# A sequence mixer and a ternary feed-forward layer on one core: Omega between the feed-forward blocks, and token sums from a context that DMAs add up in place

## The chip, the cores and the metric

One NeuronCore of a Trainium2 chip. The metric is device time in microseconds of one execution.

## What is computed

A batch of 16 sequences of 1024 tokens, 256 channels, goes through two sublayers. Cut to what matters:

```python
# mixer, on xn = layernorm(x)
omega = einsum('bsd,ed->bse', xn, W_omega) + b_omega
phi = cumsum(omega * exp(log_scale) / sqrt(position), axis=1)
cm_real, cm_imag = xn * cos(phi), xn * sin(phi)
mem_real = cumsum(cm_real, axis=1) / position
mem_imag = cumsum(cm_imag, axis=1) / position
ret_real = mem_real * cos(phi) + mem_imag * sin(phi)
ret_imag = mem_imag * cos(phi) - mem_real * sin(phi)
context = concatenate([cm_real, cm_imag, ret_real, ret_imag])   # 1024 wide
h = layernorm(context, ln_gamma, ln_beta) @ W1.T + b1           # to 512
x1 = x + xn + gelu(h) @ W2.T + b2                               # to 256
# feed-forward part, weights quantised to -1, 0, 1
out = x1 + relu(layernorm(x1) @ Wq1.T + b1) @ Wq2.T + b2        # 256 to 1024 to 256
```

## The kernel before

The tokens are cut into 32 chunks of 512, two to a sequence; sums that run over a sequence carry their last column from the even chunk to the odd one. Every fp32 operand of a matmul is split into two fp16 halves, a high one (a cast, mostly on ScalarE) and a low one (what the cast leaves, on VectorE), and TensorE multiplies both.

The program is a software pipeline written out by hand. One step `s` works on four chunks at once: `now` = s in the feed-forward part, `nxt` = s+1 in the mixer's matmuls, `ahead` = s+2 in the context (phases, cosines, running sums, products), `far` = s+3 in the first normalisation and Omega. `before` = s-1 is stored. Each engine has its own `step` that lists its work in order, and engines wait for each other by semaphores alone (`need`), so an instruction that waits holds everything behind it on its engine. Queues are in order too: SP issues loads, stores and transposing transfers; POOL issues the transfers that add to what lies at the destination (`accum_op=ALU.add`), which go through one software queue.

What the change and the prediction touch:

- TensorE's step: two quarters of the hidden layer (`hidden`), the token sums of the context (`context_stats`, L921: 64 matmuls of one column, over both halves of all eight 128-channel blocks, and L927 for the squares), the other two quarters, then `ffn_in` (L965) and `ffn_out` (L978) by blocks with a lag of three, `mixer_out` (L999), `omega` (L908) and the last three `ffn_out`.
- The mean of a token's context needs only the sum over its 1024 values; the squares come from elsewhere: POOL adds two squared tiles (`square_sums`, L534 and L536), ScalarE splits the result (`sums_hi`, L652), POOL takes the low half (`square_lo`).
- VectorE: `fraction` (L1213) takes the fractional turn that sine and cosine start from; it needs ScalarE's `whole_turns` (L608), and that the running phase sums (`phase_sums`, L1202), and those the phases (`phase_turns`, L1193) from Omega. `mixer_residual` (L1327) takes the mixer's output. `relu_lo` (L1359) is the low half that `ffn_out` waits for.
- POOL's `retrieve` (L483, L486): qa is added to rr and qb to ri by transfers of 512 KB. `output_sum` (L498) adds a chunk's result to what SP stored.
- SP's `step`: the load of x for chunk s+4, transposing transfers of `now` (rows2 to turned2) and `far` (rows1 to turned1), the store.

## Time and profile before

| | |
|---|---|
| time, median of 3 runs | 1552.74 us (1551.18 to 1555.45) |
| the profiled execution: its time, its span | 1552.36 us, 1550.6 us |
| TensorE matmuls busy | 1480.5 us, 95% |
| VectorE busy | 1395.3 us, 90% |
| ScalarE busy | 1252.0 us, 81% |
| POOL busy | 583.3 us, 38% |
| software queue (POOL's transfers), share of the 16 DMA engines | 34.9% |
| SP's queue | 19.6% |

The busy shares are sums over the span; a share of 95% leaves open who waits for whom in a step. The span is the time from the first to the last instruction, and some 2 us lie around it. The granted TensorE clock is at 0.99 of its full 2.4 GHz on the mean.

### The profile page before, as it was taken

What the parts mean: (1) busy time and instruction counts of PE and PEld (TensorE: products, weight loads), DVE (VectorE), ACT (ScalarE), POOL (GpSimd) and SP (SyncE); (2) the same over time, 40 slices, a digit from 0 to 9 for tenths busy, and PEclk for the clock granted to TensorE, in tenths of its full rate; (3) what the DMA queues carried; (4) which work ended last, traced back from release to release, by engine and by line L of the source; (5) the groups of instructions that cost most, each with busy time, mean ns of one, the idle gap of its engine ahead of it and who ended that gap; (6) DMA issues with size and microseconds to landing.
All of it is one profiled execution on the core that took longest, in us unless ns stands there. A gap on an engine that the chain in (4) does not pass through costs nothing.

```text
span 1550.6 us, 29919 instructions
## 1 busy us (share of the span) xinstructions
PE 1480.5 (95%) x10677; PEld 875.2 (56%) x10677; DVE 1395.3 (90%) x2324; ACT 1252.0 (81%) x1773; POOL 583.3 (38%) x394
## 2 busy tenths in 40 slices
PE   3689999999999999999999999999999999999997
PEld 2355555656555655555565655566555556565564
DVE  6999999999999999999999999999999999999843
ACT  6768888888987888888888897888888888889755
POOL 1323344433344443334443334444333444333421
PEclk9799999999999999999999999999999999999999
DMA  6335655555765645675555567454566555556533
GB/s 217 68 56 110 123 93 100 101 96 104 123 114 88 103 95 94 122 123 93 99 103 96 103 123 119 82 107 95 93 120 123 95 97 103 98 101 109 96 55 55
DMA packets 233603, 158.73 MB, mean 102 GB/s; under 512 B 140784, under 2 KB 223728, under 8 KB 233456
## 3 DMA queue, kind: packets, MB, share of 16 engines
q0 software_dynamic: 59376, 83.37, 34.9%
q1 hardware_dynamic: 172448, 69.77, 19.6%
q10 hardware_dynamic: 1632, 3.67, 0.6%
q8 instruction: 86, 1.41, 0.4%
q14 instruction: 61, 0.50, 0.1%
HBM read 24.13 MB, written 33.03 MB: 37 GB/s over the span
## 4 chain that ended last, share of the span: by engine, by line
PE 47%; DVE 30%; issue 9%; ACT 5%; SPq 4%; DMA 4%; DVEq 0%; ACTq 0%; POOL 0%; POOLq 0%
PE ps L978 11%; PE ps L948 11%; PE ps L999 10%; PE ps L965 8%; PE ps L908 5%; SPq L441 4%; DVE ph L1202 3%; DVE mi L1234 3%; DMA turned<-rows 2%; DVE mr L1246 2%; DVE bn L1334 2%; DVE xs L1179 2%; DVE mi L1265 2%; DVE rows L1351 2%; DVE arena L1315 2%
## 5 line engine op out<-in xcount | busy, mean ns | idle before, releaser
L948 PE MATMUL ps<-arena,w_hi 128*128 128x512 f16 x2048 | 609.0, 379 | 1.8 <-DVE arena L1291 1.1
L948 PE MATMUL ps<-arena,w_lo 128*128 128x512 f16 x1024 | 388.0, 379 | 0.0
L948 PEld LDWEIGHTS ps<-arena,w_hi 128*128 128x128 f16 x2048 | 197.8, 98 | 223.3 <-issue 2.0
L978 PE MATMUL ps<-fw_t,arena 128*128 128x256 f16 x2048 | 254.6, 272 | 11.9 <-DVE arena L1359 10.9
L965 PE MATMUL ps<-turned,fw_t 128*128 128x512 f16 x1024 | 249.1, 381 | 11.5 <-DMA turned<-rows 11.1
L978 PEld LDWEIGHTS ps<-fw_t,arena 128*128 128x128 f16 x2048 | 193.7, 97 | 94.0 <-issue 39.3
L700 ACT ACTIVATE arena<-ps,relu_bias,relu_scale 128x512 f32<-128x512 f32 x256 | 191.8, 773 | 49.0 <-PE ps L965 49.0
L534 POOL TENSOR_TENSOR sqr<-sqr,turn 128x1024 f32<-128x1024 f32 x32 | 88.5, 2765 | 334.1 <-ACT sqr L648 320.5
L1359 DVE TENSOR_TENSOR arena<-arena 128x512 f16<-128x512 f32 x256 | 170.6, 686 | 20.6 <-ACT arena L709 19.8
L999 PE MATMUL ps<-w_hi,arena 128*128 128x256 f16 x1024 | 173.2, 273 | 0.3 <-issue 0.3
L948 PEld LDWEIGHTS ps<-arena,w_lo 128*128 128x128 f16 x1024 | 100.1, 98 | 120.8
L965 PEld LDWEIGHTS ps<-turned,fw_t 128*128 128x128 f16 x1024 | 98.3, 98 | 112.7 <-DMA turned<-rows 25.0
L709 ACT CAST arena<-arena 128x512 f16<-128x512 f32 x256 | 148.6, 616 | 1.5
L999 PE MATMUL ps<-w_lo,arena 128*128 128x256 f16 x512 | 139.7, 273 | 0.0
L550 POOL TENSOR_TENSOR qa<-mi,sn 128x1024 f32<-128x1024 f32 x32 | 76.5, 2390 | 96.6 <-DVE mr L1246 86.8
L999 PEld LDWEIGHTS ps<-w_hi,arena 128*128 128x128 f16 x1024 | 100.3, 98 | 12.4 <-issue 0.7
L666 ACT ACTIVATE arena<-arena,b_full,z_down 128x512 f32<-128x512 f32 x128 | 100.4, 808 | 1.7 <-DVE arena L1315 1.3
L1320 DVE SCALAR_TENSOR_TENSOR arena<-arena,up 128x512 f16<-128x512 f32 x128 | 94.8, 744 | 0.0
L502 POOL TENSOR_TENSOR rs<-ve,minus_half 128x4 f32<-128x4 f32 x32 | 59.7, 1867 | 91.3 <-DVE ve L1345 90.5
L483 POOL DMA_DIRECT2D rr<-qa x32 | 29.8, 931 | 169.1 <-DVE rr L1281 169.1
L652 ACT CAST sqr<-sqr 128x512 f16<-128x512 f32 x32 | 19.8, 618 | 90.8 <-POOL sqr L536 90.8
L1315 DVE TENSOR_TENSOR arena<-ps,rb 128x512 f32<-128x512 f32 x128 | 82.1, 683 | 10.9 <-ACT rb L662 6.5
(184 smaller groups left out, 2783.7 us busy)
## 6 DMA issues: line engine op xcount, KB each, us to landing
x_rows<-in_L_attn_x SPq DMA_DIRECT2D x32, 512.0 KB, 4.2
rr<-qa POOLq DMA_DIRECT2D x32, 512.0 KB, 5.0
ri<-qb POOLq DMA_DIRECT2D x32, 512.0 KB, 7.1
base<-bias_rows POOLq DMA_DIRECT2D x32, 512.0 KB, 6.0
x<-bias_rows POOLq DMA_DIRECT2D x32, 512.0 KB, 8.7
out<-x SPq DMA_DIRECT2D x31, 512.0 KB, 5.5
out<-x POOLq DMA_DIRECT2D x31, 512.0 KB, 6.1
arena<-in_L_attn_W ACTq DMA_DIRECT2D x1, 2048.0 KB, 11.7
```

Of the source, the lines that this page charges most:

```text
L534: pool.tensor_tensor(sqr[:, :, :], sqr[:, :, :], turn[:, :, :], ALU.add).then_inc(q2_done, 1)
L666: act.activation(z[:, m], z[:, m], ACT.Gelu, scale=z_down[:, 0:1], bias=b1_full[:, m:m + 1])\
L700: act.activation(rf[:, m % SLOTS], ps[:, 4 + m % KE], ACT.Relu, scale=relu_scale[:, 0:1], bias=relu_bias[:, m:m + 1]).then_inc(relu_done, 1)
L709: act.copy(rh[:, m % SLOTS], rf[:, m % SLOTS]).then_inc(rh_done, 1)
L908: last = pe.matmul(ps[:, 2 + e], w[:, k, e * P:(e + 1) * P], a[:, k], start=(i == 0), stop=(i == len(passes) - 1))
L948: last = pe.matmul(ps[:, 4 + m], w[:, k, m * P:(m + 1) * P], a[:, c.b, k], start=(i == 0), stop=(i == len(passes) - 1))
L965: last = pe.matmul(ps[:, 4 + m % KE], fw1_t[:, k, m * P:(m + 1) * P], a[:, k], start=(i == 0), stop=(i == len(passes) - 1))
L978: last = pe.matmul(ps_rows_a[:, j], a[:, m % SLOTS, j * P:(j + 1) * P], fw2_t[:, m], start=(m == 0 and j % 2 == 0 and a is rh), stop=(m == ...
L999: last = pe.matmul(rows[:, j], a[:, m, j * P:(j + 1) * P], w[:, m], start=(i == 0), stop=(i == len(passes) - 1))
L1315: dve.tensor_tensor(z[:, m], ps[:, 4 + m], rb[:, :], ALU.mult).then_inc(z_done[m], 1)
L1320: dve.scalar_tensor_tensor(out=gl[:, m], in0=z[:, m], scalar=up[:, 3:4], in1=gh[:, m], op0=ALU.mult, op1=ALU.subtract).then_inc(gl_done[m], 1)
L1359: dve.tensor_tensor(rl[:, m % SLOTS], rf[:, m % SLOTS], rh[:, m % SLOTS], ALU.subtract)\
```

## The change

**Token sums.** The four parts of the context (cmr, cmi, rr, ri) are no longer summed by TensorE one after the other. POOL issues three more adding transfers of 512 KB a chunk, cmi to cmr, then rr to cmr, then ri to cmr, each of which waits for the one before. ScalarE and VectorE split the result into halves (`gathered_hi`, `gathered_lo`; they lie in qa), and TensorE sums those: 16 one-column matmuls where there were 64.

**Omega** moves from behind the mixer's output to between `ffn_in(5)` and `ffn_out(2)`.

**The order** on the other engines is rewritten. On VectorE the phases are taken between two context halves, the phase sums stand ahead of the second statistics, the carry copies stand apart, and cmr's low half comes earlier. On ScalarE `gathered_hi` and `base_scaled` stand ahead of `whole_turns`. On SP the load of x stands behind the transposes. On POOL `base_bias` comes first and `output_sum` behind `retrieve`.

**The last chunk** is transposed by TensorE straight from the normalised rows, without transposing transfers.

```diff
+        sum_halves = qa[:, :, :].bitcast(F16).rearrange("p h (k n) -> p h k n", k=KD)
+        sums_h, sums_l = sum_halves[:, 0], sum_halves[:, 1]
...
             def step(s):
-                if c := s.chunk(4):
-                    need(sp, scaled_done, c, 2)
-                    sp.dma_start(x_rows[:, c.b], x_v[c.index]).then_inc(x_loaded[c.b], 16)
...
+                if c := s.chunk(4):
+                    need(sp, scaled_done, c, 2)
+                    sp.dma_start(x_rows[:, c.b], x_v[c.index]).then_inc(x_loaded[c.b], 16)
...
+            def gather_modulated(c):
+                need(pool, cl_done[0], c)
+                need(pool, sumr_done, c)
+                need(pool, cmi_done, c)
+                pool.dma_start(cmr[:, :, :], cmi[:, :, :], accum_op=ALU.add).then_inc(gathered, 16)
+
+            def gather_retrieved(c):
+                need_sum(pool, rr_done, c)
+                need_gathered(pool, 1, c)
+                pool.dma_start(cmr[:, :, :], rr[:, :, :], accum_op=ALU.add).then_inc(gathered, 16)
+                need_sum(pool, ri_done, c)
+                need_gathered(pool, 2, c)
+                pool.dma_start(cmr[:, :, :], ri[:, :, :], accum_op=ALU.add).then_inc(gathered, 16)
...
+            def gathered_hi(c):
+                need_gathered(act, 3, c)
+                act.copy(sums_h, cmr[:, :, :]).then_inc(sums_h_done, 1)
...
                 for j in range(NT):
-                    halves = [(a, k) for k in range(KC) for a in (ch, cl)]
+                    halves = [(a, k) for k in range(KD) for a in (sums_h, sums_l)]
...
+            def last_transposes(c):
+                need(pe, xs2_done, c)
+                need(pe, x1_done, c)
+                for k in range(KD):
+                    for j in range(NT):
+                        last = pe.transpose(ps[:, 2 + k, j * P:(j + 1) * P], xs2[:, j, k * P:(k + 1) * P], ident[:, :])
+                last.then_inc(t1_done, 1)
...
                 for m in range(KF):
                     if now:
                         ffn_in(now, m, nxt)
-                        if m >= LAG:
-                            ffn_out(now, m - LAG)
+                    if m == 5 and far:
+                        omega(far)
+                    if now and m >= LAG:
+                        ffn_out(now, m - LAG)
...
                 if nxt:
                     mixer_out(nxt, now)
-                if far:
-                    omega(far)
...
+            def gathered_lo(c):
+                need(dve, sums_h_done, c)
+                dve.tensor_tensor(sums_l, cmr[:, :, :], sums_h, ALU.subtract).then_inc(sums_l_done, 1)
```

POOL's instructions around the transfers of one step, before. qa, rr and ri are the products and the retrieved parts; the sum into the output (`out<-x`) comes behind the squares (`sqr`).

```order
L550 TENSOR_TENSOR qa<-mi,sn 128x1024 [waits sumr_done,rr_done,sin_done,mi_done]
L483 DMA rr<-qa 128x1024 [waits qa_done,ra_done]
L486 DMA ri<-qb 128x1024 [waits qb_done,rb_done]
L534 TENSOR_TENSOR sqr<-sqr,turn 128x1024 [waits cl_done3,sqi_done,sqr_done]
L536 TENSOR_TENSOR sqr<-sqr 128x512 [waits q2_done]
L502 TENSOR_TENSOR rs<-ve,minus_half 128x4 [waits ve2_done]
L498 DMA out<-x 128x4x256 [waits out_done]
```

The same place of the changed kernel.

```order
L575 TENSOR_TENSOR qa<-mi,sn 128x1024 [waits rr_done,sumr_done,stats_done,sin_done,mi_done]
L491 DMA cmr<-cmi 128x1024 [waits cmi_done,sumr_done,cl_done0]
L504 DMA rr<-qa 128x1024 [waits qa_done,ra_done]
L507 DMA ri<-qb 128x1024 [waits qb_done,rb_done]
L519 DMA out<-x 128x4x256 [waits out_done]
L496 DMA cmr<-rr 128x1024 [waits gathered,rr_done]
L499 DMA cmr<-ri 128x1024 [waits gathered,ri_done]
L558 TENSOR_TENSOR sqr<-sqr,turn 128x1024 [waits cl_done3,sqi_done,sqr_done]
L560 TENSOR_TENSOR sqr<-sqr 128x512 [waits q2_done]
L511 DMA base<-bias_rows 128x4x256 [waits scaled_done]
L523 TENSOR_TENSOR rs<-ve,minus_half 128x4 [waits ve2_done]
```

The output's sum moved ahead of the squares, and the two gatherings that wait for landed transfers stand between it and them.

ScalarE's first instructions of a step, before.

```order
L652 CAST sqr<-sqr 128x512 [waits q_done]
L614 ACTIVATE x<-ps,down 128x1024 [waits stored0,xs2_done,f2_done]
L608 ACTIVATE turn<-ph,rounder 128x1024 [waits q2_done,y_done]
L581 ACTIVATE base<-x_rows,shift,gain 128x256 [waits x1_done,gain_done]
L581 ACTIVATE base<-x_rows,shift,gain 128x256 x3
L620 ACTIVATE sn<-ph 128x1024 [waits qa_done,ri_done,frac_done]
```

The same place of the changed kernel.

```order
L683 CAST sqr<-sqr 128x512 [waits q_done]
L687 CAST qa<-cmr 128x1024 [waits gathered]
L608 ACTIVATE base<-x_rows,shift,gain 128x256 [waits x1_done,gain_done]
L608 ACTIVATE base<-x_rows,shift,gain 128x256 x3
L635 ACTIVATE turn<-ph,rounder 128x1024 [waits q2_done,y_done]
L641 ACTIVATE x<-ps,down 128x1024 [waits stored0,xs2_done,f2_done]
L647 ACTIVATE sn<-ph 128x1024 [waits qa_done,ri_done,frac_done]
```

A cast that waits for the last gathering, and the scaled rows (base), came ahead of the whole turns (turn); the output copy went behind them.

TensorE's feed-forward blocks of a step, before: `ffn_in` reads turned, `ffn_out` writes by fw_t, Omega reads wo_hi and wo_lo.

```order
L965 MATMUL ps<-turned,fw_t 128x512 x16
L978 MATMUL ps<-fw_t,arena 128x256 x8
L965 MATMUL ps<-turned,fw_t 128x512 x4
L978 MATMUL ps<-fw_t,arena 128x256 x8
L965 MATMUL ps<-turned,fw_t 128x512 x4
L978 MATMUL ps<-fw_t,arena 128x256 x8
```

The same place of the changed kernel.

```order
L1017 MATMUL ps<-turned,fw_t 128x512 x16
L1030 MATMUL ps<-fw_t,arena 128x256 x8
L1017 MATMUL ps<-turned,fw_t 128x512 x4
L1030 MATMUL ps<-fw_t,arena 128x256 x8
L1017 MATMUL ps<-turned,fw_t 128x512 x4
L954 MATMUL ps<-turned,wo_hi 128x512 x4
L954 MATMUL ps<-turned,wo_lo 128x512 x2
L954 MATMUL ps<-turned,wo_hi 128x512 x4
L954 MATMUL ps<-turned,wo_lo 128x512 x2
L1030 MATMUL ps<-fw_t,arena 128x256 x8
```

Omega's twelve matmuls came in between the sixth `ffn_in` and the third `ffn_out`, ahead of the mixer's output.

## Rows read from the trace of the kernel before

**Rows 1.** The timeline of VectorE (start us, busy us, instruction [idle before <-releaser]): two residuals.

```profile
107.95 1.28 DVE L1327 SCALAR_TENSOR_TENSOR x<-ps,h_down,base 128x1024 f32<-128x1024 f32 x1
...
1479.03 1.28 DVE L1327 SCALAR_TENSOR_TENSOR x<-ps,h_down,base 128x1024 f32<-128x1024 f32 x1
```

**Rows 2.** Busy time by stretch: length, PE, PEld, DVE, ACT, POOL; clock; DMA share.

```profile
700.80:746.45 45.65, 45.24 (x330) 26.64 (x329) 42.66 (x70) 38.15 (x55) 18.22 (x13) 1.00 0.58 104
```

**Rows 3.** The timeline of TensorE in one step.

```profile
733.17 1.03 PE L978 MATMUL ps<-fw_t,arena 128*128 128x256 f16 x8 [0.28 <-DVE arena L1359]
...
746.47 1.03 PE L908 MATMUL ps<-turned,wo_hi 128*128 128x512 f16 x4
```

**Rows 4.** The chain of waits, in order of time.

```profile
716.56 1.58 PE ps L921 x64
```

**Rows 5.** The timeline of VectorE in one step.

```profile
703.62 1.41 DVE L1193 SCALAR_TENSOR_TENSOR ph<-ps,om_bias,pos_rsqrt 128x512 f32<-128x512 f32 x2 [1.23 <-PE ps L908]
...
710.62 1.23 DVE L1213 SCALAR_TENSOR_TENSOR ph<-turn,ph 128x1024 f32<-128x1024 f32 x1 [1.16 <-ACT turn L608]
...
726.49 1.92 DVE L1179 TENSOR_TENSOR xs<-qb,xs 128x1024 f16<-128x1024 f32 x1
...
732.34 0.68 DVE L1359 TENSOR_TENSOR arena<-arena 128x512 f16<-128x512 f32 x1
...
744.42 1.22 DVE L1291 TENSOR_TENSOR arena<-ri,arena 128x1024 f16<-128x1024 f32 x1
...
746.76 1.28 DVE L1327 SCALAR_TENSOR_TENSOR x<-ps,h_down,base 128x1024 f32<-128x1024 f32 x1
```

**Rows 6.** The timeline of ScalarE in the same step.

```profile
704.79 0.62 ACT L652 CAST sqr<-sqr 128x512 f16<-128x512 f32 x1 [2.75 <-POOL sqr L536]
...
709.44 1.15 ACT L608 ACTIVATE turn<-ph,rounder 128x1024 f32<-128x1024 f32 x1 [2.09 <-DVE ph L1202]
710.50 2.06 ACT L581 ACTIVATE base<-x_rows,shift,gain 128x256 f32<-128x256 f32 x4
...
718.95 1.04 ACT L631 CAST arena<-cmr 128x1024 f16<-128x1024 f32 x1 [0.41 <-DVE cmr L1220]
```

**Rows 7.** The timeline of POOL in the same step.

```profile
700.61 2.80 POOL L534 TENSOR_TENSOR sqr<-sqr,turn 128x1024 f32<-128x1024 f32 x1 [10.73 <-ACT sqr L648]
...
732.72 0.92 POOL L483 DMA_DIRECT2D rr<-qa  x1 [5.38 <-DVE rr L1281]
734.72 0.86 POOL L486 DMA_DIRECT2D ri<-qb  x1 [1.08 <-DVE qb L1275]
```

**Rows 8.** DMA, 732.8 to 743.0 us: packets, MB, share; issues with us to landing.

```profile
q0 software_dynamic: 288, 1.05, 55.1%
q1 hardware_dynamic: 1263, 0.70, 28.8%
...
rr<-qa POOLq DMA_DIRECT2D x1, 512.0 KB, 5.2
...
ri<-qb POOLq DMA_DIRECT2D x1, 512.0 KB, 7.8
```

**Rows 9.** DMA queues, 708.5 to 716.0 us.

```profile
q0 software_dynamic: 528, 0.52, 54.7%
q1 hardware_dynamic: 495, 0.50, 19.1%
```

**Rows 10.** The timeline of VectorE in the prologue.

```profile
55.59 1.21 DVE L1291 TENSOR_TENSOR arena<-cmr,arena 128x1024 f16<-128x1024 f32 x1
...
71.40 1.23 DVE L1213 SCALAR_TENSOR_TENSOR ph<-turn,ph 128x1024 f32<-128x1024 f32 x1 [1.32 <-ACT turn L608]
```

**Rows 11.** The timeline of POOL in the prologue.

```profile
53.72 1.06 POOL L483 DMA_DIRECT2D rr<-qa  x1 [1.40 <-DVE rr L1281]
```

**Rows 12.** The timeline of TensorE: an ordinary first group, and the last chunk's.

```profile
729.26 3.63 PE L965 MATMUL ps<-turned,fw_t 128*128 128x512 f16 x16
...
1530.54 5.31 PE L965 MATMUL ps<-turned,fw_t 128*128 128x512 f16 x16 [3.95 <-DMA turned<-rows]
```

More of the change, by code:

```diff
@@ L510, in step @@
                 before, now, nxt, ahead, far = s.chunk(-1), s.chunk(0), s.chunk(1), s.chunk(2), s.chunk(3)
+                if ahead:
+                    base_bias(ahead)
                 if now:
                     inverse_std_2(now)
-                if before:
-                    output_sum(before)
                 if nxt:
@@ L526, in step @@
                     product_imag_sin(ahead)
+                    gather_modulated(ahead)
                     retrieve(ahead)
+                if before:
+                    output_sum(before)
+                if ahead:
+                    gather_retrieved(ahead)
                     square_sums(ahead)
@@ L559, in _ @@
             product_imag_sin(first)
+            gather_modulated(first)
             retrieve(first)
+            gather_retrieved(first)
             square_sums(first)
@@ L713, in last_mixer @@
                 sums_hi(last)
+                gathered_hi(last)
                 output(before)
@@ L726, in last_mixer @@
                         normalise_2(last)
-                        second_hi(last)
                     relu(now, m)
                     relu_hi(now, m)
+                act.wait_ge(t1_done, 3)
+                need_block(act, f1_done, KF - 1, now)
+                act.copy(h2, ps[:, 2:4]).then_inc(h2_done, 1)
             def step(s):
@@ L743, in step @@
                     sums_hi(nxt)
+                    gathered_hi(nxt)
+                if ahead:
+                    base_scaled(ahead)
+                    whole_turns(ahead)
                 if before:
@@ L746, in step @@
                 if ahead:
-                    whole_turns(ahead)
-                    base_scaled(ahead)
                     sine(ahead)
+                    magnitude(ahead)
                 if now:
@@ L774, in step @@
                     relu(now, 0)
+                    relu_hi(now, 0)
                 if nxt:
@@ L864, in _ @@
             sine(first)
+            magnitude(first)
             cosine(first)
@@ L1370, in last_mixer @@
             def last_mixer(now, last):
+                gathered_lo(last)
                 lean_2(now)
@@ L1399, in step @@
                     return
+                if ahead:
+                    fraction(ahead)
+                if nxt:
+                    gathered_lo(nxt)
                 if now:
                     lean_2(now)
-                if ahead:
-                    fraction(ahead)
                 if far:
@@ L1422, in step @@
                 if ahead:
+                    memory_imag(ahead)
                     sums_real(ahead)
+                if far:
+                    unit_squares(far)
+                if ahead:
+                    carry_real(ahead)
                 if nxt:
@@ L1430, in step @@
                 if ahead:
+                    context_lo(ahead, 0, cmr[:, :, :])
                     memory_real(ahead)
+                    retrieve_imag_cos(ahead)
                 if nxt:
                     scale_hidden(nxt, 3)
+                if now:
+                    relu_lo(now, 0)
                 if ahead:
-                    retrieve_imag_cos(ahead)
                     retrieve_real_cos(ahead)
@@ L1448, in step @@
                     relu_lo(now, 1)
-                    relu_lo(now, 2)
                 if nxt and now:
                     gelu_lo(nxt, 0)
-                if ahead:
-                    context_lo(ahead, 0, cmr[:, :, :])
+                if now:
+                    relu_lo(now, 2)
+                if far:
+                    first_join(far)
                 if nxt and now:
@@ L1550, in _ @@
             phase_sums(first)
+            carry_phase(first)
             dve.wait_ge(p_max, 1)
@@ L1572, in _ @@
             sums_real(first)
+            carry_imag(first)
+            carry_real(first)
             dve.wait_ge(p_tab, 16)
@@ L1600, in _ @@
             phase_sums(second)
+            carry_phase(second)
             prepared(dve)
```

101 lines of the change are left out of this document (58 added, 43 removed).

## The prediction, written before the changed kernel ran

> **What bounds the kernel now.** I read the rate first. The residual of chunk 0 starts at 107.95 us and that of chunk 30 at 1479.03 us, so 30 steps take 45.70 us each [rows 1], and 30 steps are 1371 of the 1550.6 us. The step is what has to be priced.
>
> Then one step on each engine, the one that ends with the residual at 746.76. TensorE hardly waits: it is busy for 45.24 of 45.65 us, VectorE for 42.66, and the DMA engines for 0.58 of the step [rows 2]. The 64 one-column matmuls of the token sums are 1.58 us of the chain of waits [rows 4]. Omega starts right behind the mixer's output, at 746.47, and the first visible stall of the step is 0.28 us at 733.17, for VectorE's low half of relu block 0 [rows 3]. VectorE waits twice: 1.23 us for Omega (L1193) and 1.16 us for ScalarE's whole turns (L1213) [rows 5]. So the step is a loop through both: VectorE from the fraction (710.62) to the low half of relu 0 (start 732.34; 0.68 long, its successor starts after 0.60), TensorE from 733.17 through nine blocks of the feed-forward part and the mixer's output, then Omega, phases, turns, fraction. ScalarE and POOL have gaps at the step's start: ScalarE waits 2.75 us for POOL's squares and 2.09 us for the phase sums [rows 6]; POOL waits 10.73 us before its squares [rows 7].
>
> Last the transfers, because the change adds some to the software queue. Between 732.8 and 743.0 two accumulating transfers of 512 KB (rr, ri) and a store ran. The queues' shares, 55.1% and 28.8% of 10.2 us, say that rr and ri took 2.81 us of all 16 engines each, and SP's queue 2.94 us, of which I put 0.7 to the last transpose and 2.2 to the store. First packets come about 1.2 us after an issue, at 733.9; 2.81 + 2.81 + 2.94 = 8.6 us later is 742.5, and ri landed at 734.72 + 7.8 = 742.5 [rows 7, 8]. So in this stretch the work of the two queues adds up with no gap, and transfers of one queue land in their order: rr at 732.72 + 5.2 = 737.9, before ri, although ri was issued 2 us behind it. The sum into the output costs 54.7% of 7.5 us = 4.1 us, the load of x 19.1% = 1.4 us [rows 9].
>
> **The change, part by part.** I anchor the step at H, the end of the low half of relu 0 (732.94 in the step shown).
>
> *Token sums.* 48 of 64 matmuls go: 48/64 of 1.58 us = 1.2 us a step off TensorE. That is worth 1.2 us only if TensorE alone sets the step.
>
> *Added work.* ScalarE gets a cast of 1.04 us and VectorE a subtraction like L1291 (1.22 us, the next starts 1.14 later) [rows 5, 6]. Both stand at the start of the step.
>
> *VectorE, fraction to H.* Before 22.3 us (710.62 to 732.94) [rows 5]. After: +1.14 for the new subtraction, +0.14 for lean_2, which stood ahead of the fraction; the low half of cmr comes in and the product rr goes out behind H, 0. The low half of the first rows (1.92 us at 726.49, where the plain length is 1.22) overlaps POOL's product less, because the two small instructions of unit_squares (0.3 us) now stand ahead of it too; I take -0.3, bounds 0 and -0.7. With a gap of 0.18 us gone: **23.1 us**.
>
> The Trainium skill (SBUF — State Buffer, Who interferes with whom) says that a VectorE instruction with two inputs in SBUF contends with a GpSimd instruction that reads SBUF, and one blocks until the other is through. The 1.92 us at 726.49 agree with it. By the rule alone the overlap left would be about 0.5 us and the saving 0.2.
>
> *Omega at m = 5.* VectorE no longer waits for it and the phases leave the path, but its 2.6 us (12 matmuls) now stand between the low half of relu 0 and the mixer's output. Before, H to the next residual (746.76) was 13.8 us. After, +2.6, and +1.0 because relu 1's low half now stands behind two 1.14 us products and TensorE waits for it: 17.3 us. From a residual to the fraction it was 9.5 us (710.62 less 746.76 - 45.65); without the two waits (1.23, 1.16), the phases (1.33 to the next) and lean_2 (0.14) it is 5.6, with 0.3 for the copies of carries that every second step has, 5.9. This loop gives 23.1 + 17.3 + 5.9 = 46.3 us: what the Omega wait gives back, the longer way through TensorE takes again.
>
> *Squares to fraction.* The low half of ri (part 3) is through 12.6 us behind H now (744.42 + 1.14). After, rr's product is in and cmr's half out (0), the phases are in (+1.33) and one relu half more (+0.6): 14.5 us. POOL's squares then take 4.2 us until ScalarE's cast starts (700.61 to 704.79), the cast 0.55, the new cast 0.95, base_scaled 2.0 and the whole turns 1.15, with handovers 8.95 us in all [rows 6, 7]. ScalarE runs in order, so the fraction now stands behind all of it: 23.1 + 14.5 + 8.95 = 46.5 us.
>
> *The three gathering transfers.* This is the term that decides. POOL issues cmi's at about H-3.4, rr and ri at H+1.25 and H+2.5, then the sum into the output (moved here from the start of the step), then rr's gathering once rr has landed, then ri's once that one has landed, and only then the squares. Each of these waits holds POOL, and behind it stand the squares, sums_hi, base_scaled and the whole turns. In the software queue rr's gathering lies behind ri and behind the output sum. From rr's first packet at H+2.35 until it has landed the engines must move rr 2.8, ri 2.8, the output sum 4.1, the gathering 2.8, the store 2.2, and what is left of the load of x, which SP now issues behind the transposes (0.9 of 1.4 us): 15.6 us, so it lands at H+18. From there: the issue of the last gathering 0.92, and the 8.95 us above: **9.85 us**. (The last gathering itself, about 4.8 us alone, lands just ahead of the cast that needs it.) The step is 23.1 + 18.0 + 9.85 = **50.9 us**, 5.2 more than before.
>
> The Trainium skill (DMA: Bandwidth & Descriptors, Queues, rings and completion order) says that each DMA engine takes turns between the queues and consumes one queue's descriptors in order. The landings of rr and ri agree. By that rule nothing lets the gathering pass the output sum.
>
> Bounds of this term: if nothing of SP's queue fell into the stretch, 12.5 instead of 15.6 us and a step of 47.8; if all of x, and a transpose that gets pushed back by cmi's gathering, fall into it, 16.8 us and 52.1.
>
> *Start.* In the prologue cmi's gathering waits for a context half that ends near 56.8 us and holds POOL, where rr's transfer went out at about 53.7. Then two gatherings stand ahead of the squares. The first fraction, at 71.40 before, comes 8 to 10 us later [rows 10, 11]; I take +9 (bounds 4 and 12).
>
> *End.* The last chunk's halves no longer go through the transposing transfers. TensorE waited 3.95 us for them and then took 5.31 us for 16 matmuls that take 3.63 in other steps [rows 12]; its gap should fall under 1 us. With the last token sums and low half of relu 6 that waited behind the rows: -7.5 us (bounds -4 and -9).
>
> Sum: 30 x 5.2 + 9 - 7.5 = +157.5 on the profiled execution's 1552.36 us, which is 0.4 below the median: **1710 us**. Own range 1618 (step 47.8) to 1750.
>
> **The rivals.** *The queue has room* (0.18): rr's gathering lands by H+13.5, because the transfers overlap better than their shares say. Then the squares loop sets 46.5 us: 30 x 0.8 + 1.5 = 1578 (1558 to 1618). For it: over the whole step the engines are busy for only 0.58 of the time. Against: rr and ri in the rows just add up.
>
> *TensorE alone sets the step* (0.20): the other side. TensorE's stream is 45.2 of 45.65 us; less 1.2 it is 44.0, and with the small stalls 44.5. VectorE's work of 42.7 + 1.14 fits into that, now that its two waits of 2.4 us are gone. Then 30 x -1.2 + 1.5 gives 1518 (1510 to 1548). It needs rr's gathering landed by about H+11.5 and ScalarE's whole turns not behind POOL; it decides from a step under 45.6. Against: the loop through Omega gives 46.3 by the rows even without the transfers.
>
> *Nothing shows* (0.04): the loops come out at 45.7 and start and end cancel.
>
> **How the numbers follow.** The gathering's queue 0.58 (1710), room in the queue 0.18 (1578), TensorE 0.20 (1518), the same 0.04. Below 1550 lie about 0.2, above 1750 little: range 1550 to 1750. Within 0.3% of before is what a measurement of this kernel cannot tell from no change. Faster 0.20, same 0.04, slower 0.76.
>
> **What the profile after would show.** VectorE's idle before the fraction, for ScalarE's turns, near 4.6 us a step; ScalarE's before the cast of the squares; POOL waiting for transfers ahead of both gatherings; issue to landing of rr's gathering about 10 us and of ri's about 5; TensorE's one-column matmuls at 0.4 us a step; a TensorE gap of some 6 us ahead of the first output block of the feed-forward part. I am wrong if rr's gathering lands within 6 us of its issue, or if the fraction starts right behind VectorE's statistics.

## The result, and the profile after

The changed kernel takes 1775.7 us (median of 4 runs, 1774.4 to 1777.0), the kernel before beside it 1552.5 us: a ratio of 1.1448, 95% interval 1.1433 to 1.1464. The profiled execution's span is 1773.3 us against 1550.6. The prediction had the direction and the mechanism; the time is 66 us above its 1710 and 26 us outside its range.

The page of the profile after: the costliest groups (idle time ahead of them, and who ended it), then transfers with their median time from issue to landing.

```profile
L683 ACT CAST sqr<-sqr 128x512 f16<-128x512 f32 x32 | 19.8, 618 | 247.8 <-POOL sqr L560 247.8
L499 POOL DMA_DIRECT2D cmr<-ri x32 | 27.2, 850 | 314.1 <-DMA cmr<-rr 303.1
L1277 DVE SCALAR_TENSOR_TENSOR ph<-turn,ph 128x1024 f32<-128x1024 f32 x32 | 39.2, 1225 | 127.9 <-ACT turn L635 127.9
L982 PE MATMUL ps<-ident,crs 128*128 128x128 f32 x128 | 27.7, 353 | 102.3 <-POOL crs L528 102.3
...
cmr<-cmi POOLq DMA_DIRECT2D x32, 512.0 KB, 5.5
rr<-qa POOLq DMA_DIRECT2D x32, 512.0 KB, 6.3
ri<-qb POOLq DMA_DIRECT2D x32, 512.0 KB, 9.1
cmr<-rr POOLq DMA_DIRECT2D x32, 512.0 KB, 10.9
cmr<-ri POOLq DMA_DIRECT2D x32, 512.0 KB, 4.5
```

Read from the second row: POOL stood 303 us in 31 steps, ahead of its last gathering, waiting for rr's to land. Behind that stand its squares, for which ScalarE waited 248 us, and behind ScalarE's row stands the fraction, ahead of which VectorE waited 128 us.

One step of the changed kernel as one stretch; columns as in [rows 2].

```profile
721.94:774.73 52.79, 45.60 (x281) 26.00 (x280) 46.43 (x72) 39.41 (x56) 21.28 (x16) 0.97 0.64 120
```

The same step on VectorE (start, busy, [idle before <-releaser]); the first and last line are two residuals, the other four stand between them in the program's order of one step.

```profile
131.44 1.28 DVE L1399 SCALAR_TENSOR_TENSOR x<-ps,h_down,base 128x1024 f32<-128x1024 f32 x1
...
721.94 1.23 DVE L1277 SCALAR_TENSOR_TENSOR ph<-turn,ph 128x1024 f32<-128x1024 f32 x1 [5.96 <-ACT turn L635]
...
724.22 1.12 DVE L1213 SCALAR_TENSOR_TENSOR lean<-rs,mv 128x4 f32<-128x4 f32 x1
...
745.85 1.21 DVE L1349 TENSOR_TENSOR rr<-mr,cs 128x1024 f32<-128x1024 f32 x1
...
774.73 1.23 DVE L1277 SCALAR_TENSOR_TENSOR ph<-turn,ph 128x1024 f32<-128x1024 f32 x1 [3.97 <-ACT turn L635]
...
1709.15 1.28 DVE L1399 SCALAR_TENSOR_TENSOR x<-ps,h_down,base 128x1024 f32<-128x1024 f32 x1 [0.60 <-PE ps L1051]
```

On POOL:

```profile
724.05 1.27 POOL L567 TENSOR_TENSOR sqr<-sqr 128x512 f16<-128x512 f32 x1
...
742.75 0.91 POOL L491 DMA_DIRECT2D cmr<-cmi  x1 [2.52 <-DVE arena L1359]
747.93 0.85 POOL L504 DMA_DIRECT2D rr<-qa  x1 [4.27 <-DVE rr L1349]
748.74 0.91 POOL L507 DMA_DIRECT2D ri<-qb  x1
749.28 1.72 POOL L519 DMA_DIRECT2D out<-x  x1
754.77 0.88 POOL L496 DMA_DIRECT2D cmr<-rr  x1 [3.77 <-DMA rr<-qa]
765.29 0.86 POOL L499 DMA_DIRECT2D cmr<-ri  x1 [9.64 <-DMA cmr<-rr]
765.86 2.88 POOL L558 TENSOR_TENSOR sqr<-sqr,turn 128x1024 f32<-128x1024 f32 x1
```

With the prediction's anchor H at 745.85 (relu 0's low half is through, rr's product begins), the step is 23.9 us from the fraction to H, 19.4 us from H to the landing of rr's gathering at 765.29, and 9.4 us from there to the next fraction: 52.8 us, where 23.1 + 18.0 + 9.85 were predicted. Over 23 steps from the middle of the kernel the three stretches are 24.0, 19.6 and 9.4 us on the mean, 53.0 together. The transfers in the second stretch of the step shown, from rr's issue to the landing:

```profile
q0 software_dynamic: 960, 2.10, 70.3%
q1 hardware_dynamic: 1735, 1.21, 23.6%
```

Of 17.3 us that is 12.2 us of all 16 engines for the software queue (predicted 2.8 + 2.8 + 4.1 + 2.8 = 12.5) and 4.1 us for SP's queue (predicted 3.1).

Residual of chunk 0 to that of chunk 30 is 30 steps: 1577.7 us, 52.59 each, against 45.70 before [rows 1]. So the 222.7 us that the span grew are 30 x 6.89 = 206.6 of the steps, 23.5 ahead of the first residual (131.44 for 107.95) and -7.4 behind the one of chunk 30 (64.2 for 71.6). TensorE, its start, its gap inside the step, and its end:

```profile
115.68 1.89 PE L954 MATMUL ps<-turned,wo_hi 128*128 128x512 f16 x4 [15.45 <-DMA turned<-xs]
...
735.09 1.11 PE L982 MATMUL ps<-ident,crs 128*128 128x128 f32 x4 [4.08 <-POOL crs L528]
736.00 1.06 PE L996 MATMUL ps<-arena,w_hi 128*128 128x512 f16 x2
...
738.25 0.59 PE L996 MATMUL ps<-arena,w_hi 128*128 128x512 f16 x2
...
1755.03 3.61 PE L1017 MATMUL ps<-turned,fw_t 128*128 128x512 f16 x16 [0.37 <-issue]
```

The last line answers to the last of [rows 12]: the wait of 3.95 us is 0.37 now, and the 16 matmuls take 3.61 us for 5.31. After the gap of 4.08 us two matmuls take 1.06 us where the same pair takes 0.59 two microseconds later. By stretch, the gap, the 2.7 us behind it and the next 7.2:

```profile
730.80:735.00 4.20, 0.21 (x1) 0.00 (x0) 4.13 (x12) 3.86 (x6) 1.90 (x1) 0.94 0.86 125
735.10:737.80 2.70, 2.70 (x9) 1.51 (x10) 2.67 (x5) 2.49 (x3) 0.00 (x0) 0.50 0.49 97
737.80:745.00 7.20, 7.09 (x33) 2.99 (x31) 7.20 (x9) 5.54 (x9) 3.27 (x2) 0.99 0.44 88
```

The granted clock is 0.50 of full behind the gap, the 1.2 GHz level, and back at 0.99 after 2.7 us. Off the path here, it costs half of those 2.7 us of TensorE. It is not so in every step: in the next one the gap at this place is 2.35 us, and the four matmuls behind it take 0.65 us for the 1.11 us here.

### The profile page after: what moved, and what is told of

Read it like the earlier page. It is cut to its first block and busy times, and to the rows that moved or that the text cites. A ratio compares the mean times of both kernels' runs of the same rounds, so it can differ in the third digit from the quotient of the medians.

```text
span 1773.3 us, 27145 instructions
## 1 busy us (share of the span) xinstructions
PE 1514.8 (85%) x9149; PEld 857.0 (48%) x9149; DVE 1501.0 (85%) x2356; ACT 1288.3 (73%) x1805; POOL 683.4 (39%) x490
## 5 line engine op out<-in xcount | busy, mean ns | idle before, releaser
L996 PE MATMUL ps<-arena,w_hi 128*128 128x512 f16 x2048 | 652.7, 402 | 8.1 <-DVE arena L1359 6.3
L996 PE MATMUL ps<-arena,w_lo 128*128 128x512 f16 x1024 | 410.2, 401 | 0.0
L996 PEld LDWEIGHTS ps<-arena,w_hi 128*128 128x128 f16 x2048 | 208.6, 103 | 258.4 <-issue 57.3
L735 ACT ACTIVATE arena<-ps,relu_bias,relu_scale 128x512 f32<-128x512 f32 x256 | 197.4, 771 | 68.3 <-PE ps L1017 67.9
L1431 DVE TENSOR_TENSOR arena<-arena 128x512 f16<-128x512 f32 x256 | 172.4, 683 | 18.5 <-ACT arena L744 17.4
L744 ACT CAST arena<-arena 128x512 f16<-128x512 f32 x256 | 154.5, 615 | 4.3
L1017 PEld LDWEIGHTS ps<-turned,fw_t 128*128 128x128 f16 x1024 | 97.6, 98 | 115.9 <-DVE arena L1387 23.1
L499 POOL DMA_DIRECT2D cmr<-ri x32 | 27.2, 850 | 314.1 <-DMA cmr<-rr 303.1
L1277 DVE SCALAR_TENSOR_TENSOR ph<-turn,ph 128x1024 f32<-128x1024 f32 x32 | 39.2, 1225 | 127.9 <-ACT turn L635 127.9
L982 PE MATMUL ps<-ident,crs 128*128 128x128 f32 x128 | 27.7, 353 | 102.3 <-POOL crs L528 102.3
L618 ACT ACTIVATE qb<-x_rows,lean,rs 128x256 f32<-128x256 f32 x128 | 66.4, 589 | 56.2 <-issue 49.1
L954 PE MATMUL ps<-turned,wo_hi 128*128 128x512 f16 x256 | 70.9, 402 | 26.9 <-DMA turned<-xs 16.2
```

Source lines behind the costliest of these rows:

```text
L618: last = act.activation(xs[:, j], x_rows[:, c.b, j], ACT.Identity, scale=rs1[:, c.b, j:j + 1], bias=lean1[:, c.b, j:j + 1])
L735: act.activation(rf[:, m % SLOTS], ps[:, 4 + m % KE], ACT.Relu, scale=relu_scale[:, 0:1], bias=relu_bias[:, m:m + 1]).then_inc(relu_done, 1)
L744: act.copy(rh[:, m % SLOTS], rf[:, m % SLOTS]).then_inc(rh_done, 1)
L954: last = pe.matmul(ps[:, 2 + e], w[:, k, e * P:(e + 1) * P], a[:, k], start=(i == 0), stop=(i == len(passes) - 1))
L996: last = pe.matmul(ps[:, 4 + m], w[:, k, m * P:(m + 1) * P], a[:, c.b, k], start=(i == 0), stop=(i == len(passes) - 1))
L1017: last = pe.matmul(ps[:, 4 + m % KE], fw1_t[:, k, m * P:(m + 1) * P], a[:, k], start=(i == 0), stop=(i == len(passes) - 1))
```

## The experiments

Fourteen more kernels. First the table they give: the residual of chunk 0, the mean of the 30 steps to chunk 30's residual, and the rest of the span behind it, read from each profiled execution as above. Some small instructions recur in the text. rs1 and rs2 are POOL's inverse standard deviations of the two normalisations, and crs is that of the context, which TensorE spreads over the partitions. lean_2 is VectorE's product of rs2 and the mean, and ve its variance of the first normalisation that rs1 starts from; all these have 128x4 elements. square_lo is POOL's low half of the square sums, 128x512 elements. lean_2, rs2 and square_lo stand near each other at the start of a step.

| kernel | us | ratio (95%) | residual 0 | step | rest |
|---|---|---|---|---|---|
| before | 1552.5 | 1 | 107.95 | 45.70 | 71.6 |
| changed | 1775.7 | 1.1448 (1.1433-1.1464) | 131.4 | 52.59 | 64.2 |
| a1 sum early | 1737.3 | 1.1193 (1.1167-1.1220) | 132.2 | 51.30 | 64.2 |
| a2 turns first | 1792.3 | 1.1548 (1.1525-1.1570) | 130.8 | 53.17 | 64.1 |
| a3 old sums | 1595.2 | 1.0270 (1.0251-1.0289) | 112.0 | 47.22 | 65.3 |
| a5 signs first | 1768.4 | 1.1396 (1.1373-1.1419) | 123.1 | 52.66 | 64.2 |
| a6 sum last | 1888.3 | 1.2174 (1.2139-1.2208) | 131.4 | 56.36 | 64.7 |
| a8 turns and rs2 | 1698.6 | 1.0951 (1.0930-1.0972) | 131.1 | 50.06 | 64.2 |
| c1 rs2 alone | 1776.0 | 1.1449 (1.1428-1.1470) | 131.1 | 52.64 | 64.2 |
| c2 old sums, signs | 1597.1 | 1.0294 (1.0280-1.0308) | 113.3 | 47.21 | 65.3 |
| f1 squares early | 1672.8 | 1.0784 (1.0759-1.0809) | 122.4 | 49.40 | 64.2 |
| f2 and rs2 first | 1659.1 | 1.0708 (1.0669-1.0748) | 121.1 | 49.06 | 64.4 |
| b1 gathering alone | 1708.1 | 1.1005 (1.0978-1.1032) | 116.4 | 50.74 | 73.0 |
| b2 Omega alone | 1581.7 | 1.0187 (1.0164-1.0211) | 106.9 | 46.73 | 72.8 |
| b3 last chunk | 1544.8 | 0.9955 (0.9937-0.9972) | 109.0 | 45.62 | 65.2 |
| b4 gathering placed | 1595.5 | 1.0286 (1.0255-1.0317) | 110.7 | 47.32 | 64.1 |

### The parts of the change by themselves

**a3, the changed kernel with the token sums of before.**

```diff
-                    gather_modulated(ahead)          # POOL, likewise gather_retrieved
...
-                    gathered_hi(nxt)                 # ScalarE, likewise gathered_lo on VectorE
...
-                    halves = [(a, k) for k in range(KD) for a in (sums_h, sums_l)]
+                    halves = [(a, k) for k in range(KC) for a in (ch, cl)]
```

> The changed kernel without the gathering: no accumulating transfers into cmr, no halves of the sum, and the token sums again over all 64 matmuls of the eight context blocks. Everything else of the change stays (Omega inside the feed-forward loop, the new orders on all engines, the output sum behind the retrievals, the last chunk's end). Theory (the gathering transfers are what the step is lost to): the step falls from 52.6 us to between 45.2 and 46.5 us, total 1535 to 1580 us. Rival (the new orders or Omega's place cost most of it, the transfers little): the step stays above 50 us, total above 1690 us.

Measured 1595.2 us, a step of 47.2. So 180 of the 223 us leave with the gathering. The step is 0.7 us above the theory's upper end. The prediction's loop through Omega, 46.3 us, holds the new subtraction of 1.14 us, which this kernel does not have; without it the loop is 45.2, and 2.0 us are missing. Nearly all of them stand in one instruction:

```profile
736.99 1.13 DVE L1204 SCALAR_TENSOR_TENSOR lean<-rs,mv 128x4 f32<-128x4 f32 x1 [0.93 <-POOL rs L523]
```

lean_2 waits 0.93 us for rs2, which stands behind the bias of base now, and takes 1.13 us where the prediction had 0.14. From H (711.55) to the residual (728.76) it is 17.2 us in this kernel, and from there to the fraction 6.1, as predicted (17.3 and 5.9).

**b1, the kernel before with the gathering alone.**

```diff
                     retrieve(ahead)
+                    gather_modulated(ahead)
+                    gather_retrieved(ahead)
                     square_sums(ahead)
...
-                    halves = [(a, k) for k in range(KC) for a in (ch, cl)]
+                    halves = [(a, k) for k in range(KD) for a in (sums_h, sums_l)]
```

> The kernel before with the gathering alone: the three accumulating transfers behind the two retrievals and ahead of GpSimd's squares, the halves of the sum and 16 matmuls for the token sums. No other order changes; the output sum stays at the start of the step. Theory (the chain of retrieval, three gatherings, GpSimd's squares, ScalarE's turns and the fraction sets the step): 49 to 51 us, total 1650 to 1715 us. Rival (the loss needs the new orders too): step under 46.5 us, total under 1580 us.

Measured 1708.1 us, a step of 50.74, as the theory has it. Its waits, with total, times and the longest:

```profile
ACT sqr L678 <- POOL sqr L559: 275.8, 32, 12.0
POOL cmr L496 <- DMA cmr<-cmi: 220.6, 32, 8.1
...
POOL cmr L499 <- DMA cmr<-rr: 145.1, 32, 6.5
```

The chain is the same as in the changed kernel, only that here cmi's gathering goes out behind the two retrievals, and so is waited for too. The new orders are not needed for the loss.

**b2, the kernel before with Omega's place alone.**

```diff
                         ffn_in(now, m, nxt)
+                        if m == 5 and far:
+                            omega(far)
                         if m >= LAG:
                             ffn_out(now, m - LAG)
...
-                if far:
+                if far and not now:
                     omega(far)
```

> The kernel before with Omega's 12 matmuls moved between the sixth input block of the feed-forward part and the output block beside it; everything else as before. Theory (the loop fraction, relu 0, mixer output, residual becomes 1.0 to 1.2 us longer, while VectorE's wait for Omega goes): step 45.7 to 46.9 us, total 1552 to 1590 us, likeliest 1580. Rival (VectorE's two waits of 2.4 us are won): step 44.5 us, total 1515 to 1545 us.

Measured 1581.7 us, a step of 46.73: 1.03 us more, as the theory has it. VectorE from relu 0's low half to the residual:

```profile
698.33 0.69 DVE L1361 TENSOR_TENSOR arena<-arena 128x512 f16<-128x512 f32 x1 [0.43 <-ACT arena L709]
...
715.20 1.28 DVE L1329 SCALAR_TENSOR_TENSOR x<-ps,h_down,base 128x1024 f32<-128x1024 f32 x1
```

The residual is 16.3 us behind H (698.93), for 13.8 before: 2.5 us more, about what Omega's 12 matmuls take (2.6 us in the prediction). From the residual to the next fraction (723.39) it is 8.2 us for 9.5, since VectorE's wait for them (1.23 us in [rows 5]) is gone. The orders of the other engines, without the gathering, add the rest up to a3's 47.22; no run has them alone.

**b3, the kernel before with the end of the change.**

```diff
-                if c := s.chunk(0):
+                if (c := s.chunk(0)) and c.index < CHUNKS - 1:     # SP: no transposing transfers for the last chunk
...
+                        if nxt and m == KF - 3:
+                            last_transposes(nxt)                    # TensorE, 8 transposes into PSUM
```

> The kernel before with the last chunk's end of the change alone: its rows are turned on TensorE by 8 transposes into PSUM, not by the transposing transfers. Theory: what the change gave at the end, measured there as 7.4 us, is independent of the rest: total 1544 to 1547 us. Rival (half of it came from the new orders): 1548 to 1551 us.

Measured 1544.8 us, ratio 0.9955 (0.9937 to 0.9972): the rest of the span is 6.4 us shorter. Of the parts tested alone it is the one that pays, and this version beats both kernels.

### What stands in the row between rr's landing and the fraction

**a1, the output sum at the step's start; a6, the same sum behind the squares.**

```diff
                     retrieve(ahead)
-                if before:
-                    output_sum(before)                # a1: behind inverse_std_2(now); a6: behind square_sums(ahead)
-                if ahead:
                     gather_retrieved(ahead)
```

> The changed kernel, but GpSimd issues the sum into the output at the start of its step again, so it no longer stands between the retrievals and the gatherings in the software queue. Theory (the queue is served in order, and the 4.1 us of the output sum are in front of rr's gathering): rr's gathering lands about 4 us earlier, the step is 48.5 us, total about 1650 us (1630 to 1680). Rival (the transfers do not hold each other up, or another wait ends at the same time): step within 1 us of 52.6, total above 1745 us.

Measured 1737.3 us: 38 us won instead of 125. In a1's trace, VectorE's lean_2, POOL's square_lo, and the issue behind the landing of rr's gathering:

```profile
709.52 2.34 DVE L1212 SCALAR_TENSOR_TENSOR lean<-rs,mv 128x4 f32<-128x4 f32 x1
...
710.17 1.66 POOL L566 TENSOR_TENSOR sqr<-sqr 128x512 f16<-128x512 f32 x1
...
748.87 0.85 POOL L499 DMA_DIRECT2D cmr<-ri  x1 [7.81 <-DMA cmr<-rr]
```

With H at 732.37 rr's gathering has landed 16.5 us behind it, 2.9 earlier than in the changed kernel: the queue does serve the output sum first, but it was worth 2.9 us, not 4.1 (3.3 us on the mean of 23 steps, 16.3 for 19.6). From the fraction to H it is 25.1 us, 1.2 more: an instruction on 4 elements took 2.34 us and ended when POOL's square_lo did (711.86 and 711.83). From the landing to the fraction it is 0.6 us more: the second instruction of POOL's squares took 2.08 us for 1.27.

> The changed kernel with the sum into the output issued behind GpSimd's squares instead of between the retrievals and the gatherings. In the run with that sum at the step's start, rr's gathering landed 2.9 us earlier behind relu 0's low half (16.5 for 19.4 us), but 1.2 us were lost because the sum's issue pushed GpSimd's square_lo onto VectorE's lean_2, and 0.6 us in the squares. Theory (queue order): here the 2.9 us stay, step 49.6 us, total about 1685 us (1675 to 1705). Rival (what was lost there was not that overlap): total 1730 to 1745 us.

Measured 1888.3 us, beyond both. In a6 rr's gathering lands at 740.62, 16.45 us behind H (724.17), so the gain of a1 is there again. But a new wait, ahead of the residual, took all of it and more:

```profile
740.62 0.85 POOL L499 DMA_DIRECT2D cmr<-ri  x1 [7.52 <-DMA cmr<-rr]
...
751.41 1.28 DVE L1398 SCALAR_TENSOR_TENSOR x<-ps,h_down,base 128x1024 f32<-128x1024 f32 x1 [11.51 <-DMA out<-x]
```

The residual writes the buffer that the output sum of two chunks earlier still reads. I had overlooked this wait, which is in the code (added, two chunks back). It bounds how late that sum may stand.

**a2, the turns ahead of the casts; a8, the same with rs2 ahead of the bias of base; c1, rs2 alone.**

```diff
                     sums_hi(nxt)
+                if ahead:
+                    whole_turns(ahead)
+                if nxt:
                     gathered_hi(nxt)
                 if ahead:
                     base_scaled(ahead)
-                    whole_turns(ahead)
...
+                if now:                               # POOL; a8 and c1
+                    inverse_std_2(now)
                 if ahead:
                     base_bias(ahead)
-                if now:
-                    inverse_std_2(now)
```

> The changed kernel, but ScalarE rounds the phases (whole turns) right behind the cast of the square sums, ahead of the cast of the gathered sum and of base_scaled. Theory (VectorE's fraction stands behind all of ScalarE's work in a row, 1.0 + 2.0 us of it for nothing): the fraction comes 2.9 us earlier against the landing of rr's gathering, step 49.7 us, total about 1687 us (1665 to 1710). Rival (the casts are awaited by the next step's path anyway, by the token sums on TensorE): step within 1 us of 52.6, total above 1745 us.

Measured 1792.3 us, slower than the changed kernel by 17: the theory fell. Waits of VectorE in a2:

```profile
DVE lean L1215 <- POOL rs L523: 94.4, 31, 3.2
DVE ph L1279 <- ACT turn L635: 43.6, 28, 3.1
```

The fraction's wait went from 128 to 44 us, and 94 us of a new one stand behind it: lean_2 waits for rs2, which POOL computes behind the bias of base, which waits for ScalarE's base_scaled.

> The changed kernel with ScalarE's whole turns ahead of the cast of the gathered sum and of base_scaled, as in the run that came out 17 us slower, and in addition GpSimd's rs2 ahead of the bias of base, as before the change. Theory (there the fraction came earlier, but lean_2 waited 3.2 us for rs2, which GpSimd does behind the bias that waits for base_scaled on ScalarE): the wait goes, step 50 to 50.8 us, total 1700 to 1720 us. Rival (the row of ScalarE is awaited in full by something else too): total above 1760 us.

Measured 1698.6 us, a step of 50.06, the wait is gone. The row of ScalarE is worth 2.5 us a step once nothing else hangs on it. VectorE and POOL behind the fraction in a8:

```profile
742.06 0.16 DVE L1215 SCALAR_TENSOR_TENSOR lean<-rs,mv 128x4 f32<-128x4 f32 x1
...
744.05 1.46 DVE L1209 TENSOR_SCALAR ve<-mv 128x4 f32<-128x4 f32 x1
...
743.81 1.67 POOL L567 TENSOR_TENSOR sqr<-sqr 128x512 f16<-128x512 f32 x1
```

square_lo comes later here, and lean_2 is through before it in 0.16 us. Now another small instruction meets it: ve takes 1.46 us for the 0.17 of the changed kernel and ends at 745.51, square_lo at 745.48. The loss has moved with square_lo and is not gone; from the fraction to H it is 24.05 us on the mean, for 23.96.

> The changed kernel with one edit: GpSimd's rs2 ahead of the bias of base, as before the change. From fraction to relu 0's low half VectorE took 23.9 us instead of the predicted 23.1, and lean_2 in it 1.1 us instead of 0.14. Theory (rs2, held by the bias that waits for base_scaled, is late for lean_2 by 0.8 to 1.0 us in each step): step 51.6 to 51.8 us, total 1745 to 1753 us. Rival (lean_2 is only held by GpSimd's other work and the chain ends with rr's gathering in any case): 1770 to 1782 us.

Measured 1776.0 us, no change: the theory fell. lean_2 still takes 1.12 us in c1, for square_lo is in progress. In the changed kernel's rows above it is the same: lean_2 from 724.22 to 725.34, POOL's square_lo from 724.05 to 725.32. So the 0.8 us are not rs2's lateness but POOL's square_lo beside it. In 30 steps of the changed kernel lean_2 overlaps it and takes 1.12 us; in a8, where it does not, it takes 0.16. rs2's order is no matter of its own here; it is where the fraction comes earlier (3.2 us of waiting in a2, 0.93 in a3).

### Can the gathering be placed so that it costs nothing?

**f1, and f2 with one edit more.** From the changed kernel, with the edits of a1, a2 and a5, and:

```diff
-                    gather_retrieved(ahead)
+                    gather_real(ahead)                # rr's gathering
                     square_sums(ahead)
+                    gather_imag(ahead)                # ri's gathering
...
+                    gathered_hi(nxt)                  # ScalarE, behind magnitude(ahead)
+                    gathered_lo(nxt)                  # VectorE, ahead of modulate_imag(ahead)
...
+                    inverse_std_2(now)                # f2 alone: rs2 and the output sum ahead of base_bias
```

> The changed kernel with its gathering, Omega and end kept and its orders mended: GpSimd's squares stand between rr's gathering and ri's, the output sum is issued at the step's start, ScalarE rounds the phases right behind the cast of the squares and casts the gathered sum behind the absolute values, VectorE subtracts it just ahead of the product cmi, and Omega of the first step stands behind the signs. Theory (only the waits for the transfers in front of the squares made it slow): step 46.5 to 47.5 us, total 1575 to 1615 us. Rival (the added traffic itself, three transfers of 2.8 us of all engines, slows the retrievals and the transposes by as much): step above 49 us, total above 1660 us.

> The mended order of the run at 1672.8 us (squares between the gatherings, whole turns first, output sum at the start, Omega of the first step behind the signs), in addition with GpSimd's rs2 and the output sum ahead of the bias of base. There lean_2 waited 2.4 us for rs2 in every step and all gatherings were off the path. Theory: step 49.4 - 2.4 = 47.0 us, total about 1600 us (1590 to 1625). Rival (another of the added instructions is late next, the subtraction of the gathered sum or the token sums): total above 1640 us.

f1 took 1672.8 us and f2 1659.1 us, steps of 49.40 and 49.06. Both theories fell, and both times lie in the range of the rival. The traces do not show what f1's rival says, though (that the added traffic slows the retrievals and the transposes). The stretches behind H are nearly those of a3, which has no gathering: H to the residual 17.3 and 17.2 us, and from there to the fraction 6.3. The loss stands from the fraction to H, with 25.9 and 25.6 us on the mean, for 23.7 in a3. No gathering is waited for on the way to the squares any more. In f1 lean_2 waited 2.41 us for rs2; f2 left 0.93 us of it and won 0.3 us a step only. In f2, VectorE's product cmi and POOL's rs1 beside it:

```profile
724.34 2.17 DVE L1299 TENSOR_TENSOR cmi<-xf,sn 128x1024 f32<-128x1024 f32 x1
...
723.37 4.01 POOL L485 TENSOR_TENSOR rs<-ve,minus_half 128x4 f32<-128x4 f32 x1
```

The product takes 1.22 us when alone; POOL's power of 4 elements takes 1.95 us elsewhere in the same kernel. Both are in each other's way: POOL's small work, square_lo (3.30 us there, 1.15 in b4) and rs1, falls into VectorE's dense stretch. So f2's rival holds in this: other work is late next, but it is this small work, neither the subtraction nor the token sums.

**b4, the kernel before with b3's end and the squares between the last two gatherings as in f1.** cmi's gathering stands behind the two retrievals, and the cast of the sum behind the sine. Omega and all other orders as before.

> The kernel before with the last chunk's end of the change, and the gathering placed off the path: rr's gathering ahead of GpSimd's squares, ri's behind them, the cast of the sum behind ScalarE's sine, its subtraction ahead of VectorE's product cmi, 16 matmuls for the token sums. Omega and all other orders as before. Theory (gathering costs only where it holds the squares; what is left is 1.1 us of VectorE and some waits): step 46 to 47.5 us, total 1553 to 1600 us. Rival A (TensorE sets the step, 1.2 us of matmuls are won): total under 1540 us, below the 1544.8 us of the end alone. Rival B (the traffic itself costs): above 1640 us.

Measured 1595.5 us: 50.7 us more than b3. The step is 47.32, 1.70 more than b3's. The subtraction that was added, in b4:

```profile
740.19 1.23 DVE L1355 TENSOR_TENSOR qa<-cmr,qa 128x1024 f16<-128x1024 f32 x1 [0.62 <-ACT qa L690]
```

1.14 us to the next plus 0.62 of waiting is 1.76, and from the fraction to H it is 24.1 us on the mean for 22.4 in b3. So a gathering off the path costs what it adds to VectorE, and the 1.2 us of TensorE's matmuls bring nothing.

### The start

**a5, in the first step Omega behind the signs; c2, that in a3.**

```diff
-                    if m == 5 and far:
+                    if m == 5 and far and now:
                         omega(far)
...
                     mixer_out(nxt, now)
+                if far and not now:
+                    omega(far)
```

> The changed kernel, but in the first step only, which has no feed-forward part, TensorE does Omega behind the transposes of the weights' signs and the mixer's output, as before. Theory (15 us of the start were lost because TensorE waited for the transposing transfers of chunk 2 with this work behind it): the residual of chunk 0 comes at about 117 us instead of 131.4, total 14 us less, about 1762 us. Rival (the start was lost to the gatherings of chunk 0 and 1 alone): no change, 1772 to 1779 us.

> The changed kernel without the gathering (as in the run at 1595.2 us) and with Omega of the first step behind the signs. Theory (without gathering, Omega's place in the first step is the whole of the 4.0 us by which chunk 0's residual is later than in the kernel before): residual of chunk 0 at 108 to 109 us, step 47.2 us as without this edit, total 1590 to 1593 us. Then the 6.7 us that were left open at the start come from the gathering and the new orders together. Rival (the orders themselves delay the start): residual at 111.5 us or later, total 1594 to 1597 us.

a5: 1768.4 us, chunk 0's residual at 123.1 for 131.4, so 8.3 us given back, not 14. c2: residual at 113.3, step 47.21, 1597.1 us: the rival, since a3 had 112.0 without the edit. The start therefore sums as: orders 5.3 us (c2), gathering 8.5 (b1), Omega ahead of the signs with the gathering in the queue 8.3 (a5), together 22.1 of 23.5. The 1.4 us left are put to their meeting, which no run isolates.

## Why the prediction was right in direction and 66 us short

Three terms of the sum failed. The one for the stretch from H to the landing of rr's gathering (18.0 us) was taken without the transpose that cmi's gathering pushes back, and came to 19.6 us. The one from the fraction to H (23.1 us) took lean_2 as free, and came to 23.9 us. The one for the start (+9 us) put Omega's new place and the new orders at nothing there, and came to +23.5 us.

- **The three gatherings hold POOL, and the squares, ScalarE's row and the fraction hang on it:** right, shown by a3 and b1. Rivals "the queue has room" (1578) and "TensorE alone" (1518) are out: rr's gathering took 10 to 11 us from issue to landing, and b4 shows that TensorE's saving brings nothing even when the transfers are off the path.
- **H to the landing, 18.0 us predicted, 19.4 measured (19.6 on the mean of 23 steps).** The mis-sized term. The step shown is not a usual one: there rr's transfer went out 2.1 us behind H, and SP's queue put 4.1 us into the stretch. In the next step, as in nearly all, it went out at H+1.5 (799.96, H at 798.45), near the H+1.25 that I had, and up to the landing at 818.08 it is 12.4 us of all engines for the software queue (predicted 12.5) and 4.7 for SP's queue (predicted 3.1). A transpose and all of the load of x fell into it, which was my upper bound and not my value. The runs show why. The issue of the four transposes, in the changed kernel, in a3 without the gathering, and in b1 with cmi's gathering behind the retrievals:

```profile
741.42 6.76 SPq L453 DMA_TRANSPOSE turned<-xs  x4
...
754.20 5.12 SPq L453 DMA_TRANSPOSE turned<-xs  x4
...
757.89 5.11 SPq L456 DMA_TRANSPOSE turned<-xs  x4
```

  It is 6.7 to 6.9 us in nearly all steps of every kernel that issues cmi's gathering 1.3 us behind the first of them, and 5.1 in nearly all steps of those that do not (b1 and b4 issue it some 9 us later). I had this as a bound, "a transpose that gets pushed back by cmi's gathering". "Nothing lets the gathering pass the output sum" held; a1 and a6 price it at 2.9 us in the steps shown.
- **Fraction to H, 23.1 predicted, 23.9 measured.** I took lean_2 at 0.14 us. It stands now where POOL's square_lo runs and took 1.12 us (c1); in a8 the loss moved with square_lo to another small instruction. The Trainium skill (SBUF — State Buffer, Who interferes with whom), which the prediction applied to the first rows, says that a VectorE instruction with two SBUF inputs and a reading GpSimd instruction exclude each other for a whole instruction; the ends 725.34 and 725.32 of lean_2 and square_lo agree. I had looked for it at the big instruction only.
- **Landing to fraction, 9.85 predicted, 9.4 measured.** Right.
- **These make 52.8 for 50.9 us.** Over 30 steps the mean is 52.59, and 1.7 x 30 is 51 us of the error.
- **Start, +9 predicted, +23.5 measured.** The gathering alone costs 8.5 (b1), as I had it. What failed is that I priced nothing else there: Omega stands at m = 5 also in the first step, where there is no feed-forward part to fill the time, and TensorE waited 15.45 us for transposes with the weights' signs behind it. That is 8.3 us (a5); the new orders are 5.3 (c2), which I had at nothing, and 1.4 are left.
- **Omega's loop 46.3 us predicted, 47.2 measured (a3), which has no subtraction, so 45.2 is what to compare.** Its parts through TensorE and back to the fraction held; lean_2 is what the 2.0 us are. (The terms 13.8, 2.6 and 1.0 add to 17.4, not 17.3.) **End, -7.5 predicted, -7.4 measured,** 6.4 of it by the last chunk's transposes alone (b3).
- **Where TensorE would wait** was wrong: not ahead of the first output block, but ahead of the spread (L982), for POOL's crs: 102 us. It is off the path; TensorE was idle for 7 us of the step shown.
- Adding up, measured less predicted: +1.4, +0.8 and -0.4 us in the step shown, 14.5 us at the start, nothing at the end. The range's upper end of 1750 allowed 52.1 for the step and 12 for the start; both ends were passed.

## What to carry to other kernels

A saving on the busiest engine (here 1.2 us of 45.7) is worth nothing when two engines' orders close a loop of the same length; what is moved onto the other engine is paid in full. An engine that issues transfers in order must not hold a wait for one of them in front of work that others wait for, and in one queue count everything issued earlier, to the landing, and what a new transfer does to the transposes beside it. When an instruction is moved, ask for its neighbour on POOL too, and look at the first iteration by itself: what fills a wait in the steady state is not there yet.

## What the runs showed of the hardware that was not expected

- VectorE's lean_2 on 128x4 elements took 0.14 to 0.17 us in nearly all steps in which it did not overlap square_lo. It took 1.12 us beside it in the changed kernel and 2.34 us in a1, and both ended together. The phases' scan of two took 2.33 us in one step of the changed kernel and 4.82 us beside the squares in c1. Its size did not protect an instruction; what POOL was in decided.
- Four transposing transfers took 6.7 to 6.9 us to issue with an accumulating transfer issued 1.3 us behind the first, and 5.1 us in nearly all steps without one.
- Taking a transfer that moves 4.1 us of all engines out from in front of another one brought that one 2.9 us forward in the steps shown of two kernels, and 3.3 and 3.2 us on the mean of 23 steps.
- An accumulating transfer of 512 KB within the chip landed 4.5 us after its issue when last in the queue (ri's gathering), and 10 to 11 us (rr's) with ri's transfer, the output sum, a store and a load of x in flight.
